# First round of a graph kernel: the copies of attr go from VectorE to GpSimd

## The reference

```python
for t in range(num_rounds):
    src = x[row]
    dest = x[col]
    m_input = jnp.concatenate([dest, src, edge_attr], axis=1)
    messages = m_input @ msg_W[t].T + msg_b[t]
    agg = jax.ops.segment_sum(messages, row, num_segments=x.shape[0])
    x = _gru_cell(agg, x, gru_Wih[t], gru_bih[t], gru_Whh[t], gru_bhh[t])
```

## Time and profile before

| what | value |
|---|---|
| median of 3 runs | 2363.29 us (2361.75 to 2366.62) |
| span of the profiled execution | 2356.6 us, 6.7 below the median of the runs |
| VectorE busy in the span | 2175.2 us (92%) |
| ScalarE busy | 1953.9 us (83%) |
| TensorE matmuls busy | 1597.8 us (68%) |
| GpSimd busy | 658.3 us (28%) |
| first copy of attr, last one (start) | 710.4 us, 1533.0 us |

### The profile page before, as it was taken

How to read it: one execution, slowest core, us unless ns; L and a number is a source line. 1 busy time by engine, 2 the same in 40 slices (tenths; PEclk the granted TensorE clock), 3 DMA queues, 4 the chain that set the end, 5 groups by cost and what they waited for, 6 DMA issues and landing times. The chain is left out here.

```text
span 2356.6 us, 126105 instructions
## 1 busy us (share of the span) xinstructions
PE 1597.8 (68%) x46870; PEld 1496.5 (64%) x46870; DVE 2175.2 (92%) x3629; ACT 1953.9 (83%) x4429; POOL 658.3 (28%) x853
## 2 busy tenths in 40 slices
PE   0000000000148899999999999959999999999996
PEld 0000000000138899999999999948899999999996
DVE  7999999999279899999999999958899999999996
ACT  4777895563248899999999999959899999999996
POOL 1000000000553444454544444511222222222222
PEclk9999999999959999999999999979999999999998
DMA  6100001211436666666677766647677777777773
GB/s 124 25 0 0 0 0 31 50 23 23 116 93 210 209 227 226 228 227 230 226 232 226 228 224 226 221 144 227 218 246 249 245 248 248 247 245 246 250 247 122
DMA packets 176134, 400.90 MB, mean 170 GB/s; under 512 B 73499, under 2 KB 77505, under 8 KB 175571
## 3 DMA queue, kind: packets, MB, share of 16 engines
q1 hardware_dynamic: 117047, 202.53, 27.1%
q0 software_dynamic: 57296, 195.19, 25.1%
q10 hardware_dynamic: 1708, 2.10, 0.3%
HBM read 384.73 MB, written 14.67 MB: 169 GB/s over the span
## 5 line engine op out<-in xcount | busy, mean ns | idle before, releaser
L1286 ACT ACTIVATE rows<-ps_rows 128x512 f16<-128x512 f32 x2744 | 1436.3, 647 | 47.2 <-PE ps_rows L1187 36.0
L1397 DVE TENSOR_TENSOR src<-iota_units,src_lane 128x2048 f16<-128x2048 f16 (+1 forms) x784 | 861.6, 1099 | 17.2 <-PE ps_sum L1205 13.7
L1207 PE MATMUL ps_sum<-rows,src 128*64 128x132 f16 x10976 | 585.6, 223 | 20.7 <-ACT rows L1286 14.0
L1187 PE MATMUL ps_rows<-rows_next,planes 128*64 128x128 f16 x10976 | 551.0, 220 | 32.9 <-DVE planes L1387 23.2
L1187 PE MATMUL ps_rows<-rows_now,planes 128*64 128x128 f16 x10976 | 559.8, 219 | 17.8 <-DVE planes L1387 7.8
L1205 PE MATMUL ps_sum<-src,rows 128*64 128x128 f16 x10976 | 563.9, 221 | 7.5 <-issue 6.4
L1387 DVE TENSOR_SCALAR planes<-planes,lane_no 128x2048 f16<-128x2048 f16 (+1 forms) x784 | 532.2, 679 | 5.6 <-DMA planes<-lanes_dram 5.3
L1187 PEld LDWEIGHTS ps_rows<-rows_now,planes 128*64 128x64 f16 x10976 | 425.2, 110 | 38.4 <-ACT rows L1286 14.4
L1187 PEld LDWEIGHTS ps_rows<-rows_next,planes 128*64 128x64 f16 x10976 | 412.3, 110 | 56.8 <-DVE planes L1387 23.9
L890 PE MATMUL ps_src<-ident,late 112*64 112x112 f32 x98 | 21.2, 394 | 607.3 <-DVE late L962 586.9
L1207 PEld LDWEIGHTS ps_sum<-rows,src 128*64 128x64 f16 x10976 | 404.8, 110 | 34.4 <-ACT rows L1286 21.5
(11 more groups left out here) (203 smaller groups left out, 2044.0 us busy)
## 6 DMA issues: line engine op xcount, KB each, us to landing
planes<-lanes_dram POOLq DMA_DIRECT2D x294, 512.0 KB, 4.8
planes<-lanes_dram SPq DMA_DIRECT2D x291, 512.0 KB, 4.6
planes<-lanes_dram POOLq DMA_DIRECT2D x98, 256.0 KB, 4.1
planes<-lanes_dram SPq DMA_DIRECT2D x97, 256.0 KB, 3.9
rows_now<-parts_dram SPq DMA_DIRECT2D x112, 32.0 KB, 1.7
rows_next<-parts_dram SPq DMA_DIRECT2D x112, 32.0 KB, 4.0
parts_dram<-rows_now SPq DMA_DIRECT2D x1, 3136.0 KB, 16.2
sorted_dram<-planes SPq DMA_DIRECT2D x1, 3136.0 KB, 11.6
```

Of the source, the lines that this page charges most:

```text
L1187: last = nc.tensor.matmul(ps_rows[(u + NU * b) % 4][half * SLOTS:(half + 1) * SLOTS, k * 2 * H:(k + 1) * 2 * H], dst1[q][:, (c - q * QC) * ...
L1207: last = nc.tensor.matmul(ps_sum[b][at, 0:width], hot[:, at], row, start=(j == 0), stop=(j == J - 1))
L1286: nc.scalar.activation(rows[:, (u + NU * b) % ring, 0:n, 0:2 * H], cut(ps_rows[(u + NU * b) % 4][:])[:, 0:n, :], ACT.Copy).then_inc(rows_r ...
L1397: nc.vector.tensor_tensor(src1[q][:, 0:pairs_now], iota_units[:].rearrange("p (o l) k -> p o l k", o=1) .broadcast_to([P, pairs_now, P, 2] ...
```

## The change

GpSimd makes the copies of attr. Behind the issue of the lanes of tile s, quarter q, its queue gets a wait for `scattered` and the copy for tile s - 1, quarter q, with a semaphore of its own, `attr_put`; behind the last tile's lanes it makes the copies of the last tile. TensorE waits for `attr_put` beside `src1_ready` before the first scatter of a quarter. VectorE's copy goes. The second round is the same.

```diff
+            attr_put = path_sem(f"attr_put{r}") if r == 0 else None
...
                 for q in range(NQ):
                     engine.wait_ge(dst1_ready, (s - 1) * NQ + q + 1)
                     fetch_some_lanes(engine, s, r, q)
+                    if r == 0:
+                        put_attr(engine, s - 1, q)
+
+            def put_attr(engine, s, q):
+
+                units = units_of(q)
+                wait(engine, scattered, done_with(s, q))
+                plain(nc.gpsimd.tensor_copy(
+                    rows[:, units[0]:units[-1] + 1, :, 2 * H:2 * H + 2].rearrange("p u k v -> p (u k) v"),
+                    attr_two[:, bass.ds(s, 1), units[0] * UJ:(units[-1] + 1) * UJ, :]
+                    .rearrange("p o j v -> p (o j) v"))).then_inc(attr_put, 1)
...
                     in_pairs(pool, NT, body, DEEP)
+                    for q in range(NQ):
+                        if r == 0:
+                            put_attr(pool, NT - 1, q)
                     for k in range(NT - 2, NT):
                         copy_now(k, k % 2)
...
                             te.wait_ge(src1_ready, s * NQ + q + 1)
+                            if r == 0:
+                                te.wait_ge(attr_put, s * NQ + q + 1)
...
                         units = units_of(q)
-                        if r == 0:
-                            nc.vector.tensor_copy(
-                                rows[:, units[0]:units[-1] + 1, :, 2 * H:2 * H + 2].rearrange("p u k v -> p (u k) v"),
-                                attr_two[:, bass.ds(s, 1), units[0] * UJ:(units[-1] + 1) * UJ, :]
-                                .rearrange("p o j v -> p (o j) v"))
                         pairs_now = len(units) * UJ // 2
```

## The result

| | median us | runs |
|---|---|---|
| before, same chip | 2364.26 | 5, 2361.75 to 2374.78 |
| after | 2346.49 | 5, 2340.54 to 2352.99 |
| after / before | 0.9918 | 95% interval 0.9894 to 0.9942 |

Faster by 0.8%, some 18 us, where 8 were forecast. The profiled execution of after took 2346.05 us, with a span of 2344.4. The same lines have new numbers: L1387 is now L1404 (dst one-hot), L1397 L1409 (src one-hot), L1419 to L1429 L1431 to L1441 (node work), L1455 L1467, L1207 L1224, L1115 L1127; the puts are L1074.

What follows compares the result with a forecast made beforehand. VectorE's queue was taken to lead the first round: -0.225 us for copies and +0.14 for puts give -0.085 us per tile, over 98 tiles taken as -8 us, so 2355 us; range 2333 to 2375.

Steps and rivals of the forecast that it cites:

- the copy fits into that wait: First quarter: src one-hot waits for GpSimd's lanes issue, so removing VectorE's copy gains 0, bounds 0 and 0.13 us.
- the 0.8 that the prediction named as its sign: First quarter after the change: src one-hot still some 0.8 us behind its dst one-hot, against 0.66 in second and third.
- The row of the second round: Src one-hot at 1908.20, no copy before it, starts 0.09 us before a GpSimd DMA issue ends; read as waiting for it.
- a put at 0.035 us: Each GpSimd copy of attr takes 0.035 us from VectorE, bounds 0 and 0.25; four make 0.14 us per tile.
- The row of 0.04 us: GpSimd copy ending at 1008.50 met L1422, whose next start came after 0.11 us against 0.07: 0.04 us lost.
- Rival 1: Slower: each put holds VectorE for its whole length, 0.25 us; +76 us, 2439; chance 0.08.
- Rival 2: Slower: puts delay the first quarter's lanes past the 0.6 us left, each second tile; +26 us, 2389; chance 0.11.
- Rival 3: No change: puts at 0.04 to 0.07 us each give all back, 2359 to 2368; chance 0.28.
- Rival 4: Faster by all: puts cost nothing, first quarter's 0.13 us gained too; 0.355 us per tile, -35 us, 2328; chance 0.10.
- ScalarE's 0.37 us: ScalarE's spare time per tile in the first round; a VectorE gain beyond it would make ScalarE the next limit.
- GpSimd's added work: 392 copies at 0.6 us add 235 us to GpSimd's 658.3, staying below half of the span.
- TensorE's wait of 0.1 us for the first put: Before the first quarter's first scatter TensorE may stand some 0.1 us in every second tile; costed at nothing.

Runs made afterwards that it cites:

- e1: Kernel before with nobody copying attr, its two columns zeroed once and its sums left out: 2335.5 us, 0.9887 of before.
- e4: Changed kernel with only the second to fourth quarters' copies on GpSimd, the first back on VectorE: 2349.87 us, 0.9937 of before.
- e3: Changed kernel with only the first quarter's copy on GpSimd, the other three back on VectorE: 2359.53 us, 0.9974 of before.
- e2c: Kernel before with all VectorE copies kept, GpSimd making the same 392 copies into a spare buffer nobody reads: 2369.39 us, 1.0005 of before.
- e9: Changed kernel with GpSimd's node copy moved behind the second quarter's put, run beside the unaltered changed kernel: 2339.81 us, 0.9883 of before.
- e10: Kernel before with nobody copying attr and GpSimd's node copy moved as behind the second quarter's put: 2333.9 us, 0.9854 of before.
- e5: Changed kernel with each put cut into two of half the units, 784 GpSimd copies in place of 392: 2347.75 us, 0.9915 of before.
- e6: Changed kernel with each put ahead of the lanes' issue and not behind it: 2346.19 us, 0.9893 of before.
- e8: Changed kernel, unaltered, run again in the same rounds as the version with the node copy moved: 2352.06 us, 0.9923 of before.
- e7: Changed kernel with GpSimd's node copy moved from behind the fourth quarter's put to behind the second's, first run: 2337.95 us, 0.9868 of before.

## Why the prediction was right or wrong

**Right: the sign and the bound.** VectorE's queue leads the first round, and what leaves it shortens the tile: 0.26 us per tile, by which ScalarE's wait for `new_rest` fell from 28.3 to 0.9 us. The time lies in the range, at 2346.5 against a forecast of 2355. It owes that to the width of the range (2333 to 2375) and not to the sum: the sum had 0.085 us per tile, and 0.260 came. The two errors below both made the gain too small, and that the first 20 tiles gained nothing hid a part of them.

**Wrong: "the copy fits into that wait", the first quarter's copy at 0.** This is the step that failed. The prediction saw a src one-hot that starts 0.09 us before a DMA issue ends and another that does so in the second round, and took both for a wait for that issue. In after, e1 and e4 the one-hot starts 0.20, 0.19 and 0.11 us before the issue ends, and in after it comes 0.664 us behind its dst one-hot, not the 0.8 that the prediction named as its sign. e3, with that copy alone moved, gained 0.119 us per tile. What it was worth is the 0.13 us that the prediction had as its upper bound.

The row of the second round did show a wait, but for TensorE: for `scattered`, which the src one-hot needs. Two such places in the second round of after, in order of time, and TensorE's scatter at the place of the earlier trace rows in before (last line):

```profile
1847.27 0.74 DVE L1404 TENSOR_SCALAR planes<-planes,lane_no 128x2048 f16<-128x2048 f16 x1
1847.49 0.73 POOL L1146 DMA_DIRECT2D out_dram<-out_rows  x1 [0.69 <-POOL out_rows L1143]
1847.51 0.40 PE L1222 MATMUL ps_sum<-src,rows 128*64 128x128 f16 x8
1848.06 1.22 DVE L1409 TENSOR_TENSOR src<-iota_units,src_lane 128x2048 f16<-128x2048 f16 x1
...
1862.63 0.74 DVE L1404 TENSOR_SCALAR planes<-planes,lane_no 128x2048 f16<-128x2048 f16 x1
1862.85 0.73 POOL L1146 DMA_DIRECT2D out_dram<-out_rows  x1 [0.69 <-POOL out_rows L1143]
1862.99 0.42 PE L1222 MATMUL ps_sum<-src,rows 128*64 128x128 f16 x8
1863.57 1.22 DVE L1409 TENSOR_TENSOR src<-iota_units,src_lane 128x2048 f16<-128x2048 f16 x1 [0.20 <-PE ps_sum L1222]
...
1907.61 0.43 PE L1205 MATMUL ps_sum<-src,rows 128*64 128x128 f16 x8
```

The issue starts 0.22 us and ends 0.95 us behind the dst one-hot in both, and yet the src one-hot starts 0.79 us behind it in the one and 0.94 in the other. What it keeps is its distance from the end of TensorE's scatter, some 0.15 us in both and at 1908.20 in before. In one tile of this stretch of before (2076.66) the issue comes 1.7 us behind the dst one-hot, and the src one-hot still starts 0.84 behind it. So that row was no second case of the first quarter's copy: its pair of instructions was the same, its wait another.

**Mis-sized: a put at 0.035 us.** In after four puts cost 0.076 us per tile against e1, 0.019 each, and 0.018 in e2c, outside the first quarter's copy. Most of the 0.076 lies in the node work. With the node copy moved a put costs 0.008 (e9 less e10). The row of 0.04 us that the prediction leaned on showed the node copy's meeting with the small operations, worth 0.04 us by itself (e1 less e10); a put costs less.

So per tile: forecast -0.225 + 0.14 = -0.085; measured -0.336 (e1) + 0.076 = -0.260. Of the difference of 0.175 us, 0.111 is the copies (the first quarter's 0.13 that was put at nothing, less some 0.02 that came back elsewhere) and 0.064 the puts.

**Rival 1, the port held for a whole put (+76 us):** fallen. e2c adds the puts and nothing else, 0.033 us per tile; e5 doubles their number, and its pair is 0.01 us longer.

**Rival 2, late lanes (+26 us):** fallen. VectorE waits 1.8 us for lanes in 620 us, and 3.0 and 2.9 where e5 and e6 press on that margin.

**Rival 3, no change:** fallen, as the interval shows.

**Rival 4, faster by all (-35 us):** its mechanism was the true one, all four copies on the path. After stays short of it by the puts' 0.076 us, and by tiles 10 to 20, which lost 2.9 us (below). e1, without any puts, reached 0.9887, some 27 us, and e9 0.9883. e10's tile, 0.377 us shorter than before, shows that ScalarE's 0.37 us was not yet a wall.

**Smaller steps.** GpSimd's added work (235 us forecast, 228.6 measured) hides, as said. TensorE's wait of 0.1 us for the first put did not show: in tiles 20 to 96 that put ends 0.25 us or more before the scatter starts. L1115 got shorter behind the fourth put, as expected; that this pair of copies would stretch the node work was in no step.

**Open.** In tiles 10 to 20 after took 87.7 us and before 84.8. In that stretch, the waits of after (total us, times, longest us):

```profile
DVE src L1409 <- PE ps_sum L1224: 6.6, 7, 1.3
...
PE ps_sum L1224 <- issue: 3.0, 3, 1.8
```

VectorE waits there for TensorE, whose scatter stood for nothing that the profile shows; before has 0.8 us of that wait in its stretch, once, at the copy L1392. e8 has the same as after, 6.7 us. Why, no run here tells. Also not settled: the time ahead of the first round, 709.7 to 716.6 us over the profiles, which varies whichever kernel runs, and that of the first ten tiles, 82 to 91 us. The two of 91 are e7 and e10, both with the node copy moved, but e9, the kernel of e7 again, took 84; so the move by itself is not shown to cost that, and e9 did not lose the 7 us that its expectation asked after.

## What to carry to other kernels

When one engine's queue leads, every instruction in it counts from start to start, and an instruction that seems to sit in the shadow of a neighbour's wait should be written off as free only when the end of that wait, read in many tiles, moves the neighbour's start with it. Here two starts lay 0.09 us ahead of an issue's end, and neither waited for it: the second followed the end of a scatter, which the same rows show. A small copy on an engine beside it was nearly free, but not everywhere: a put and the node copy back to back against three small VectorE operations made the tile 0.08 us longer than with the node copy in another place (after less e9). So where a moved operation lands matters more than that it was moved: look which neighbours it then ends beside, and move the neighbour if it need not be there.

## What the runs showed of the hardware

- When a GpSimd copy starts within a VectorE one-hot, GpSimd waits: a put of 0.21 to 0.23 us lasts 1.08 at the median within a src one-hot, 0.43 within a dst one-hot (after), and its end falls some 0.1 us into VectorE's next instruction. VectorE pays 0.008 us per put in the mean (e9 less e10) to 0.019 (after less e1).
- A very short operation can take nearly twice its time beside GpSimd copies. L1422, on 128x1 elements, gives way after 0.070 us when no GpSimd copy is near (e9, e10), after 0.115 beside one node copy (before, e1), 0.135 beside a put and a node copy (after).
- A DMA issue on GpSimd of 0.74 us did not delay the VectorE one-hot that started beside it (after, e1, e4), nor the one in the second round: the one-hot of the earlier trace rows starts some 0.15 us behind the end of the scatter that it needs.
